# A transformer layer on one core: the rotated queries of a pair of heads turned by one DMA transpose

## What is computed

```
q = rmsnorm(x @ w_qa, q_norm_w) @ w_qb
q = q.reshape(B, L, H, DN + DR)                 # L = 512, H = 16, DN = 128, DR = 64
q_nope, q_rope = (q[..., :DN], q[..., DN:])
...
q_rope = q_rope * cos + rotate_half(q_rope) * sin
k_rope = k_rope * cos + rotate_half(k_rope) * sin
q = jnp.concatenate([q_nope, q_rope], axis=-1)
k = jnp.concatenate([k_nope, k_rope], axis=-1)
scores = jnp.einsum('blhd,bmhd->bhlm', q, k) * scale    # causal mask, softmax, @ v, @ w_o
```

## Time and profile before

| | |
|---|---|
| median of 3 runs | 1381.97 us (1381.57 to 1382.5) |
| the profiled execution's own time | 1380.98 us, with a span of 1379.2 us from first to last instruction |
| attention pairs | 166.9 to about 977 us of the span |
| PE busy over the whole span | 1052.4 us, 76% |
| DVE busy | 1100.2 us, 80% |
| ACT busy | 539.6 us, 39% |
| POOL busy | 237.3 us, 17% |
| granted TensorE clock | 0.911 of full speed over the span |

### The profile page before, as it was taken

How to read it: one execution, slowest core, us unless ns; L and a number is a source line. 1 busy time by engine, 2 the same in 40 slices (tenths; PEclk the granted TensorE clock), 3 DMA queues, 4 the chain that set the end, 5 groups by cost and what they waited for, 6 DMA issues and landing times.

```text
span 1379.2 us, 27210 instructions
## 1 busy us (share of the span) xinstructions
PE 1052.4 (76%) x7460; PEld 634.8 (46%) x7460; DVE 1100.2 (80%) x2984; ACT 539.6 (39%) x1225; POOL 237.3 (17%) x475
## 2 busy tenths in 40 slices
PE   1635587898988989989989999999652643447998
PEld 0423354555555555555555555555241322224554
DVE  5679587888888887987988888888169788886886
ACT  1549434443333434334333434344023330534443
POOL 1000012121121112112112112111003323122111
PEclk9659899999999999999999999999875766778999
DMA  9100022332322242222342232344560110000001
GB/s 361 47 1 0 1 58 56 62 61 53 58 51 55 57 116 53 57 51 48 61 116 48 56 60 55 60 118 75 163 214 9 52 31 0 0 0 8 30 38 46
DMA packets 199345, 85.73 MB, mean 62 GB/s; under 512 B 173560, under 2 KB 184824, under 8 KB 198784
## 3 DMA queue, kind: packets, MB, share of 16 engines
q1 hardware_dynamic: 199296, 85.12, 25.2%
HBM read 35.80 MB, written 7.34 MB: 31 GB/s over the span
## 4 chain that ended last, share of the span: by engine, by line
issue 35%; PE 27%; DVE 22%; POOL 8%; ACT 5%; DVEq 1%; DMA 1%; ACTq 1%; POOLq 0%; SPq 0%
PE bank L1778 5%; PE bank L1662 4%; DVE arena L1427 3%; PE bank L1728 3%; DVE arena L1444 2%; DVE arena L1451 2%; POOL arena L431 2%; PE bank L1763 2%; PE bank L1746 1%; PE bank L1750 1%; PE bank L1747 1%; POOL arena L1035 1%; PE bank L1749 1%; PE bank L1748 1%; DVE scal L1545 1%
## 5 line engine op out<-in xcount | busy, mean ns | idle before, releaser
L1173 ACT ACTIVATE arena<-bank,arena,scal 128x128 f32<-128x128 f32 (+3 forms) x256 | 157.8, 616 | 370.2 <-POOL arena L1031 370.2
L1778 PE MATMUL bank<-arena 128*128 (+1 forms) x768 | 180.7, 380 | 21.8 <-DVE arena L1457 10.8
L1451 DVE SCALAR_TENSOR_TENSOR arena<-arena 128x128 f16<-128x128 f32 (+3 forms) x256 | 169.3, 661 | 9.1
L1427 DVE TENSOR_REDUCE arena<-bank 128x1 f32<-128x128 f32 (+3 forms) x256 | 124.3, 486 | 52.9 <-PE bank L1751 51.1
L1031 POOL TENSOR_TENSOR arena<-arena,scal 128x1 f32<-128x1 f32 x256 | 48.5, 190 | 574.5 <-DVE arena L1427 574.5
L1728 PE MATMUL bank<-arena 128*128 (+1 forms) x576 | 136.5, 383 | 0.5 <-DVE arena L1483 0.5
L1763 PE MATMUL bank<-arena 128*128 128x512 f16 (+3 forms) x768 | 117.0, 303 | 19.3 <-DMA arena<-arena 10.7
L1778 PEld LDWEIGHTS bank<-arena 128*128 (+1 forms) x768 | 72.5, 97 | 102.0 <-issue 40.2
L1444 DVE TENSOR_SCALAR arena<-arena 128x128 f16<-128x128 f32 (+3 forms) x256 | 109.7, 429 | 5.6 <-DVE arena L1436 0.8
L1763 PEld LDWEIGHTS bank<-arena 128*128 (+1 forms) x768 | 69.2, 98 | 62.9 <-issue 26.0
L1746 PE MATMUL bank<-arena 128*128 (+4 forms) x256 | 77.7, 304 | 10.1 <-ACT arena L1173 3.6
(11 more groups left out here) (213 smaller groups left out, 2114.7 us busy)
## 6 DMA issues: line engine op xcount, KB each, us to landing
arena<-in_L_attn_w_qb SPq DMA_DIRECT2D x1, 4608.0 KB, 23.7
arena<-in_x SPq DMA_DIRECT2D x4, 1024.0 KB, 5.8
arena<-in_L_attn_w_o SPq DMA_DIRECT2D x1, 4096.0 KB, 34.0
arena<-arena SPq DMA_TRANSPOSE x256, 2.8
arena<-in_fside_BxS2xS SPq DMA_DIRECT2D x4, 1024.0 KB, 5.7
arena<-in_L_ffn_w SPq DMA_DIRECT2D x8, 512.0 KB, 7.6
out<-arena SPq DMA_DIRECT2D x16, 256.0 KB, 2.0
arena<-in_x SPq DMA_DIRECT2D x12, 256.0 KB, 3.0
```

What stands on the lines that cost most here:

```text
L1173: act.activation(pf(k), banks[S_BANKS[g % 3]][:, 0:n], ACT.Exp, bias=NB[:, k:k + 1], scale=sc_exp, accum_out=SUM[:, k:k + 1]).then_inc(s_e ...
L1427: dve.tensor_reduce(NEGM[:, (g & 3):(g & 3) + 1], banks[S_BANKS[g % 3]][:, 0:n], AX.X, ALU.max, negate=True).then_inc(s_max, 1)
L1451: dve.scalar_tensor_tensor(out=ph_part(k, 1), in0=pf(k).rearrange("p (t c) -> p t c", c=P), scalar=R4[:, k:k + 1], in1=ph_part(k, 0), op0= ...
L1778: last = pe.matmul(banks[Y_BANK][:, :], ot(gp, a, k, (q & 3) * P, P), wo(b, gp * GH + k), start=(k == 0 and n == 0), stop=(k == GH - 1 and ...
```

## The change

The high and the low part of the rotated queries now stand side by side in one tile `RHL` of 12 blocks, heads outermost (8 blocks high, 4 blocks low), and one DMA transpose from SP (`turn_queries`) writes them straight to `QR`. The twelve TensorE transposes of a pair and the two DVE copies out of PSUM go, and so do four semaphores; the DVE products of `rotate` and the subtraction on POOL write in the order of heads. `turn_queries(i + 1)` stands in SP's stream after `turn_probs(i, 4)`; that of pair 0 stands ahead of the first `turn_probs`.

```diff
-        RH = take(TB * 2 * 2 * DR, fp16)
+        RHL = take(3 * L, fp16)
...
-        RL = take(TB * 2 * DR, fp16)
...
+            def turn_queries(i):
+
+                sp.wait_ge(r_split, i + 1)
+                if i >= 2:
+                    sp.wait_ge(s_mm, 8 * i - 8)
+                par = i & 1
+                sp.dma_start_transpose(QR[:, par * 1536:(par + 1) * 1536].rearrange("p (t q) -> p t q", t=12),
+                                       RHL).then_inc(r_in, 16)
+
             load_xt(TB)
+            turn_queries(0)
             for i in range(NPAIR):
                 for g in range(8):
                     turn_probs(i, g)
+                    if g == 4 and i + 1 < NPAIR:
+                        turn_queries(i + 1)
...
             def rope_split(i):
                 pool.wait_ge(r_hi, i + 1)
-                v = RH.rearrange("p (a k d) -> p a k d", k=2, d=DR)
-                pool.tensor_tensor(RL.rearrange("p (a d) -> p a d", d=DR),
-                                   RT1.rearrange("p (a d) -> p a d", d=DR), v[:, :, 0, :], ALU.subtract)\
-                    .then_inc(r_split, 1)
+                low = RHL[:, 2 * L:3 * L].rearrange("p (t h d) -> p h t d", h=2, d=DR)
+                whole = RT1.rearrange("p (h t d) -> p h t d", h=2, d=DR)
+                high = RHL[:, 0:2 * L].rearrange("p (h t k d) -> p h t k d", h=2, t=TB, k=2)
+                pool.tensor_tensor(low, whole, high[:, :, :, 0, :], ALU.subtract).then_inc(r_split, 1)
...
             def rope_hi(i):
                 act.wait_ge(r_sum, i + 1)
                 if not (isinstance(i, int) and i == 0):
-                    act.wait_ge(r_tl, i)
+                    act.wait_ge(r_in, 16 * i)
...
-                dve.tensor_tensor(RT1, q, c, ALU.mult)
...
+                dve.tensor_tensor(RT1.rearrange(by_head, h=2, d=DR), q.rearrange(by_tile, h=2, d=DR),
+                                  c.rearrange(by_tile, h=2, d=DR), ALU.mult)
...
-            def rope_out_hi(i, par):
-                dve.wait_ge(r_th, i + 1)
-                dve.tensor_copy(QR[:, par * 1536:par * 1536 + 1024], bank16[R_BANK]).then_inc(r_teh, 1)
-
-            def rope_out_lo(i, par):
-                dve.wait_ge(r_tl, i + 1)
-                dve.tensor_copy(QR[:, par * 1536 + 1024:(par + 1) * 1536],
-                                bank16[Q_BANK][:, 0:L]).then_inc(r_tel, 1)
...
             def rope_mm(i, prep=None):
...
-                    pe.wait_ge(r_teh, i)
+                    pe.wait_ge(r_rot, i)
...
-            def rope_t_hi(i):
-                pe.wait_ge(r_hi, i + 1)
...
-            def rope_t_lo(i):
-                pe.wait_ge(r_split, i + 1)
...
             def scores(i, j, g):
...
                 if g == 0:
-                    pe.wait_ge(r_teh, i + 1)
-                    pe.wait_ge(r_tel, i + 1)
+                    pe.wait_ge(r_in, 16 * i + 16)
                     pe.wait_ge(kr_te, 4 * (i >> 3) + 4)
```

More of the change, by code:

```diff
@@ L176, in decoder_layer @@
         pv_mm, o_hi, o_lo, qn_mm, qn_hi, qn_lo = (sem(n) for n in ("pv_mm", "o_hi", "o_lo", "qn_mm", "qn_hi", "qn_lo"))
-        r_mm, r_rot, r_sum, r_hi, r_split, r_th, r_tl, r_teh, r_tel = (
-            sem(n) for n in ("r_mm", "r_rot", "r_sum", "r_hi", "r_split", "r_th", "r_tl", "r_teh", "r_tel"))
+        r_mm, r_rot, r_sum, r_hi, r_split, r_in = (
+            sem(n) for n in ("r_mm", "r_rot", "r_sum", "r_hi", "r_split", "r_in"))
         y_mm, y_added, xa_in, xa_out = sem("y_mm"), sem("y_added"), sem("xa_in"), sem("xa_out")
@@ L1186, in rope_hi @@
                 if not (isinstance(i, int) and i == 0):
-                    act.wait_ge(r_tl, i)
-                v = RH.rearrange("p (a k d) -> p a k d", k=2, d=DR)
+                    act.wait_ge(r_in, 16 * i)
+                v = RHL[:, 0:2 * L].rearrange("p (a k d) -> p a k d", k=2, d=DR)
                 act.activation(v[:, :, 1, :], RT1.rearrange("p (a d) -> p a d", d=DR), ACT.Copy)
@@ L1469, in rotate @@
                 q, (c, s) = banks[R_BANK][:, :], (ROPE[:, 0:512], ROPE[:, 512:1024])
-                dve.tensor_tensor(RT1, q, c, ALU.mult)
[L1471 to L1475, removed]
-            def rope_out_hi(i, par):
-                dve.wait_ge(r_th, i + 1)
-                dve.tensor_copy(QR[:, par * 1536:par * 1536 + 1024], bank16[R_BANK]).then_inc(r_teh, 1)
-            def rope_out_lo(i, par):
-                dve.wait_ge(r_tl, i + 1)
-                dve.tensor_copy(QR[:, par * 1536 + 1024:(par + 1) * 1536],
-                                bank16[Q_BANK][:, 0:L]).then_inc(r_tel, 1)
+                by_tile, by_head = "p (t h d) -> p t h d", "p (h t d) -> p t h d"
+                dve.tensor_tensor(RT1.rearrange(by_head, h=2, d=DR), q.rearrange(by_tile, h=2, d=DR),
+                                  c.rearrange(by_tile, h=2, d=DR), ALU.mult)
+                by_tile, by_head = "p (t h k d) -> p t h k d", "p (h t k d) -> p t h k d"
+                q4, s4 = (a.rearrange(by_tile, h=2, k=2, d=DR // 2) for a in (q, s))
+                t4 = RT2.rearrange(by_head, h=2, k=2, d=DR // 2)
+                dve.tensor_tensor(t4[:, :, :, 0, :], q4[:, :, :, 1, :], s4[:, :, :, 0, :], ALU.mult)
+                dve.tensor_tensor(t4[:, :, :, 1, :], q4[:, :, :, 0, :], s4[:, :, :, 1, :], ALU.mult)\
+                    .then_inc(r_rot, 1)
             def add_y(q):
@@ L1495, in pair @@
                 for g in range(8):
-                    if g == 7 and not last:
-                        rope_out_hi(i + 1, 1 - j)
                     row_max(G + g, g)
@@ L1512, in pair @@
                         qn_lo_(2 * i + 2, 0)
-                    if g == 7 and not last:
-                        rope_out_lo(i + 1, 1 - j)
                     if prep is not None and j == 0:
@@ L1580, in _ @@
             rotate(0)
-            rope_out_hi(0, 0)
-            rope_out_lo(0, 0)
             qn_lo_(0, 0)
@@ L1674, in prep_t2 @@
                 if i is not None:
-                    pe.wait_ge(r_teh, i + 1)
+                    pe.wait_ge(r_rot, i + 1)
                 for a in range(3):
@@ L1722, in nope_mm @@
                     pe.wait_ge(qn_lo, Hd)
-                if h == 1 or (isinstance(i, int) and i == 0):
-                    pe.wait_ge(r_tel, i + 1)
                 k = 0
@@ L1803, in pair @@
                             nope_mm(i + 1, 0)
[L1804 to L1807, removed]
                     if g == 7:
@@ L1831, in _ @@
             rope_mm(0)
-            rope_t_hi(0)
-            rope_t_lo(0)
             nope_mm(0, 0)
```

2 lines of the change are left out of this document (removed).

## The result

The changed kernel takes 1422.7 us in the median of 4 runs (1417.75 to 1424.72), beside 1381.77 of the kernel before in the same series. The ratio is 1.029, with a 95% interval of 1.026 to 1.032. The forecast was 1389, with a range of 1372 to 1404 and slower as the likeliest side. The side was right, the size was not: +41 us came where about +7 had been worked out.

What follows compares the result with a forecast made beforehand. PE is close to full, and the next pair's first scores would wait for the new DMA. Gaps +7.5 us and start -1 give +6.5 on 1380.98: 1387.5, plus 1.0 for the median, about 1389; range 1372 to 1404.

Steps and rivals of the forecast that it cites:

- what fills the gap: From step 4's transpose start on SP to the next pair's first scores: a chain through the new DMA, 5.2 us.
- what costs nothing: Rotation's new write order, POOL's subtraction and step 5's later transpose: delayed or reordered, counted at nothing.
- Rival 1: 12-block transfer: quicker into a contiguous tile, gap 4.35 us, about -20 us, 1362; chance 0.12.
- a gain of 0.42 us each: Ends of pairs 8, 12, 16, 20, 24, 28: gap falls from 5.62 us, -0.42 each, -2.5 together.
- only ahead of pair 0: Start: scores 2.4 us earlier, but PE idles about 5 us and may run at half clock; taken as -1 us.
- A: Follow-up theory, not in the prediction: the queries arrive late and the waits for them are the whole loss.
- C: Follow-up theory, not in the prediction: much of the loss is TensorE's clock, which falls after stretches of idling.
- Early and late pairs: Ends of pairs 0, 2, 4, 5: +0.2 us together; of pairs 1, 3, 26, 29, 30: +3.6.
- the 0.3 each that I took off for DVE: Pairs 1, 3, 26, 29, 30: DVE, not PE, holds the next start, so +5.1 us became +3.6.
- The stores: Pairs 12, 20, 28: a 1 MB store precedes step 4's transpose and delays the queries, +2.6 us together.
- Rival 3: 12-block transfer lands later, or back-to-back transposes hold each other: landing 4.5 us, +28 us, 1417; chance 0.14.
- Rival 2: The wait for the queries never binds, so PE's and DVE's savings show: -26 us, about 1355; chance 0.06.

Runs made afterwards that it cites:

- the run with 12 dummies: Changed kernel plus 12 unread identity transposes per pair on PE, 8 at g = 6 and 4 at g = 7: 1405.07 us, ratio 1.018.
- 24 dummies: Changed kernel plus unread PE transposes, 24 at g = 6 of even pairs, 8 of odd pairs, 4 at g = 7 of all: 1405.04 us, ratio 1.017.

## Why the prediction was right on the side and wrong on the size

**Right: what fills the gap.** Step 4's issue, then the issue, the transfer, the step to PE. Forecast 1.17 + 0.05 + 3.6 + 0.36 = 5.2 us; measured in odd pairs 1.27 + 3.73 + 0.67 = 5.67. The landing of 12 blocks was extended from 8 by size and rate, and came within 0.13 us in most pairs; six of the 32 took 4.2 to 4.7 us. Each part was a little short, and the largest miss is the last: I took 0.36 from a place behind the loops, and the odd pair ends a turn of a loop, where it is 0.67. Eleven odd pairs cost +10.9 us at full clock (the run with 12 dummies) where +4.7 was forecast.

**Right: what costs nothing.** The rotation's new order, POOL's subtraction and the later step transposes: the part from scores 3 to step 4 moved by 0.8 us in 31 pairs, and in the kernel with the added DMA alone it moved as much (11.28 in odd pairs), so not even that is the new order's. Rival 1, a quicker transfer into a contiguous tile, is out: the row of the changed kernel's DMA from 647 to 651 us, the 12 blocks and behind them the 4 of step 5, shows the old rate:

```profile
GB/s 0 1 1 0 0 0 0 15 138 205 225 212 223 205 192 228 195 220 215 223 215 220 192 174 215 220 200 233 215 236 205 223 169 32 0 0 0 0 0 0
```

The 350 to 400 GB/s that the Trainium skill ("DMA: Bandwidth & Descriptors", "Latency and other measured facts") gives for a contiguous transpose are not seen here; it is about 215, contiguous or not.

**Wrong: "That is the new gap wherever it is longer than what PE and DVE need, and PE and DVE need less: at most the old gap less 0.65."** This step gave the pairs that divide by four a gain of 0.42 us each. Behind PE's transposes there stood another wait in those pairs, the projection's for `out_lo`, 1.72 us in pair 16 of the kernel before. PE's savings in front of it went straight into it: it grew to 3.54. At full clock the gap stays at 5.57, against 5.62 before. In pairs 0 to 3 the next wait was another one, that of the product with the values for step 3's transpose, and it took what the wait for L1190 gave back (no such wait stood there before):

```profile
PE bank L1740 <- DMA arena<-arena: 13.5, 4, 4.7
```

I had read the wait that would vanish and not the next one behind it.

**Wrong: no term for the clock.** The prediction looked for the clock only ahead of pair 0. There the low clock came as forecast: behind 7.12 us of idling `nope_mm` takes 3.22 us in place of 2.11 in the kernel before. But pair 0 is only 0.3 us longer, and its first scores came 3.9 us earlier, where 2.4 had been reckoned before the clock, since POOL had the low part ready at 159.15 and not at 160.52. In the stage of the pairs, where the sum had no such term, the mean granted clock fell from 0.99 to 0.94. The size of it: at full clock the late arrival costs about 10.9 in odd pairs, 0.4 in pairs 6, 10, 14, 18, 22 and 6 to 8.5 in pairs 0 to 5, 26, 29 and 30 (all from the run with 12 dummies; in the last group it added 8.5, of which 2.2 lie in the first parts of pairs 4 and 26, again at the lower clock), and about 2 in those that divide by four (gaps with 24 dummies: 0.7 and 1.2 more in pairs 12 and 20, which hold the stores). That is some 20 to 22 of the 44 us; the other 22 to 24 go with the clock. It is an estimate, since the parts come from two runs; the 25 us that PE is longer busy with the wait than without it are of the same size. The dummies gave back 17.6. The two are not rivals: the waits make both, and taking the wait away takes both away, as the run with the transpose ahead of step 4's shows. That is why A's numbers came true wherever the wait was removed or added, and C's only where PE was filled while the wait stood.

**Sizes of the smaller terms.** Early and late pairs: forecast +3.8, measured +8.9 in the changed kernel and +8.5 with the 12 dummies; the transposes issued in pairs 3 and 4 landed after 4.2 to 4.7 us, and the gaps of the late pairs grew by what the chain asks for, so the 0.3 each that I took off for DVE was not there. The stores: forecast +2.6, about +2.

Rival 3, "slower by more", gave 1417, near the measured time by luck: it asks for a landing of 4.5 us, and the median is 3.8. Rival 2's time without the wait, 1355, was measured as 1354.0, in the run that leaves the wait out.

## What to carry to other kernels

When work on an in-order engine is replaced by a transfer, write down the whole chain to its reader: what is ahead of it in the issuing queue, its issue, its landing and the step into the waiting engine. Here one place earlier in the queue decided between 3% slower and 1.7% faster. Ask for each saving on an engine which wait stands next behind it, since the saving ends there. And where TensorE is close to full, price a new wait twice: once as it stands, and once again for the matmuls behind it that may run at the lower clock.

## What the runs showed of the hardware that I had not expected

- Idle stretches of 1.8 us at the ends of pairs and 3.5 us within them, in a stage where PE is busy for nearly nine tenths, were followed by matmuls at 1.2 GHz: 9 in 3.58 us in place of 2.11, 12 in 5.30 in place of 2.76. The idling just ahead doesn't decide it: 1.7 us had the full clock behind it in the kernel before and the lower one in the kernel with the added wait, and 3.5 us had the lower one in the changed kernel and the full one with the transpose ahead of step 4's. The Trainium skill ("TensorE: Matmul & The Clock Gate", "HAM oscillation — how this bites in real kernels") tells of a kernel whose waits for a DMA made every next batch of matmuls start slow; the trace agrees in kind, and here dummy transposes worth 0.65 us of stream a pair won 17.6 us.
- A DMA transpose from SP holds the queue about 1.2 us for 2 to 8 blocks and 1.3 to 1.5 for 12, and 12 blocks land 3.7 to 3.8 us after the issue began in most pairs of the changed kernel (the longest of 32: 4.7, and its longest issue 2.7).
